# SP's loop over tile pairs written out in a four-layer graph network

## The reference

```python
# layer 0: softmax aggregation
m = relu(feat[src]) + 1e-7
a = exp(m - segment_max(m, dst)[dst]);  a = a / segment_sum(a, dst)[dst]
out = (feat + segment_sum(a * m, dst)) @ W + b
# layer 1: messages
edge_feat = mlp(edge_attr, W_edge, ...)          # relu, then a norm over all edges
message = mlp(concat([x[src], x[dst], edge_feat]), W_msg, ...)
out = segment_sum(message, dst) + mlp(x, W_node, ...)
# layers 2 and 3: two mean convolutions each, relu or elu between
agg = segment_sum(x[src], dst) / max(degree, 1)
out = agg @ Wl.T + b + x @ Wr.T
```

## Time and profile before

| | |
|---|---|
| median of 3 runs | 5197.18 us (5192.36 to 5201.1) |
| profiled execution, its own time | 5191.9 us |
| its span, first to last instruction | 5190.1 us |
| TensorE busy | 3237.4 us (62%) |
| VectorE busy | 2697.6 us (52%) |
| GpSimd busy | 2510.4 us (48%) |
| ScalarE busy | 1566.9 us (30%) |
| SP's hardware queue q1 | 239330 packets, 586.35 MB |
| mean traffic | 153 GB/s |

### The profile page before, as it was taken

How to read it: one execution, slowest core, us unless ns; L and a number is a source line. 1 busy time by engine, 2 the same in 40 slices (tenths; PEclk the granted TensorE clock), 3 DMA queues, 4 the chain that set the end, 5 groups by cost and what they waited for, 6 DMA issues and landing times.

```text
span 5190.1 us, 69196 instructions
## 1 busy us (share of the span) xinstructions
PE 3237.4 (62%) x18737; PEld 2376.6 (46%) x18737; DVE 2697.6 (52%) x5882; ACT 1566.9 (30%) x3677; POOL 2510.4 (48%) x2580
## 2 busy tenths in 40 slices
PE   1555555554656666556666664111159999999999
PEld 0333333333544444444444443100037777788777
DVE  4888888888545555555555556400001254433333
ACT  1777777775222222222222222100000011111000
POOL 7666666665466666666666666777720000000000
PEclk9999999999756766766676776555579999999999
DMA  5555555554134444444444443100037656676776
GB/s 182 191 196 194 194 195 195 194 196 153 48 93 110 113 115 114 113 110 115 114 110 112 117 112 91 60 0 0 13 113 283 224 209 246 246 254 247 260 277 227
DMA packets 387448, 796.21 MB, mean 153 GB/s; under 512 B 207412, under 2 KB 264600, under 8 KB 361128
## 3 DMA queue, kind: packets, MB, share of 16 engines
q1 hardware_dynamic: 239330, 586.35, 33.7%
q0 software_dynamic: 82320, 90.28, 8.2%
q10 hardware_dynamic: 65718, 118.62, 6.0%
HBM read 581.03 MB, written 213.92 MB: 153 GB/s over the span
## 4 chain that ended last, share of the span: by engine, by line
PE 28%; issue 19%; SPq 10%; another core or an unknown queue 7%; DVE 4%; ACT 2%; DMA 1%; ACTq 1%; DVEq 0%; POOL 0%
PE ps L1169 17%; PE ps L1099 6%; SPq L634 6%; ACT ps L1218 1%; PE ps L923 1%; SPq L609 1%; PE ps L930 1%; PE ps L929 1%; SPq L604 1%; SPq L625 1%; PE ps L1052 1%; DMA attr<-attr_parts 1%; SPq L615 1%; SPq L630 1%
## 5 line engine op out<-in xcount | busy, mean ns | idle before, releaser
L780 POOL DMA_INDIRECT area<-src_table,early x784 | 752.4, 960 | 480.1 <-remote 249.0
L780 POOL DMA_INDIRECT area<-relu_table,early x784 | 741.5, 946 | 413.2 <-issue 210.0
L941 PE MATMUL ps<-ident,area 96*128 96x96 f32 x2352 | 428.6, 348 | 429.6 <-issue 212.5
L1169 PE MATMUL ps<-second,area 128*128 128x288 bf16 x5194 | 650.7, 286 | 0.2 <-DVE second L1811 0.2
L941 PEld LDWEIGHTS ps<-ident,area 96*128 96x128 f32 x2352 | 347.6, 208 | 547.3 <-issue 402.8
L1169 PEld LDWEIGHTS ps<-second,area 128*128 128x128 f16 x5194 | 508.2, 98 | 127.7 <-DVE second L1811 0.5
L1632 DVE SCALAR_TENSOR_TENSOR second<-second,area,ps 128x512 bf16<-128x512 f32 x784 | 537.9, 741 | 0.0
L1664 DVE TENSOR_TENSOR_SCAN area<-flags,area,ps 96x512 f32<-96x512 int8 x196 | 250.0, 1276 | 534.3 <-ACT dump L1222 456.9
L929 PE MATMUL ps<-ident,area 128*96 128x128 f32 x1568 | 430.9, 370 | 112.4 <-issue 74.1
L929 PEld LDWEIGHTS ps<-ident,area 128*96 128x96 f32 x1568 | 335.8, 241 | 297.5 <-issue 246.7
L845 POOL DMA_INDIRECT adj<-out_ring x390 | 396.9, 1018 | 126.2 <-issue 126.2
(11 more groups left out here) (330 smaller groups left out, 4701.9 us busy)
## 6 DMA issues: line engine op xcount, KB each, us to landing
area<-adj SPq DMA_DIRECT2D x147, 1632.0 KB
area<-adj SPq DMA_DIRECT2D x55, 1568.0 KB
adj<-early SPq DMA_DIRECT2D x102, 816.0 KB
soft_sums<-out_ring ACTq DMA_DIRECT2D x196, 384.0 KB
second<-key_dram SPq DMA_DIRECT2D x98, 512.0 KB
area<-dst_table SPq DMA_DIRECT2D x784, 48.0 KB
sums<-out_ring ACTq DMA_DIRECT2D x196, 192.0 KB
second<-caps_dram SPq DMA_DIRECT2D x98, 192.0 KB
```

What stands on the lines that cost most here:

```text
L780: pool.indirect_dma_start(out=src_rows[:, s, c % CH, :], out_offset=None, in_=gather_table[p], in_offset=bass.IndirectOffsetOnAxis(ap=src_ ...
L941: last = nc.tensor.transpose(ps[:, b, c * F:(c + 1) * F], r[:, (s * CH + c) * P:(s * CH + c + 1) * P], ident[0:F, 0:F])
L1169: last = nc.tensor.matmul(bank(b, P, PARTS_F), slots[:, lane, s, :], y[:, s, :, :].rearrange("p c f -> p (c f)"), start=s == 0, stop=s == ...
```

## The change

In both passes the loop of SP is a Python loop, so that its 48 rounds are written out in SP's program, with constant addresses and constant counts in its waits. `load` itself is the same, and so are the programs of the other engines.

```diff
@@ -646,7 +646,7 @@
                     sp.wait_ge(later_stored, 16 * LATER_STORES)
                     sp.wait_ge(deg_made, 1)
                     sp.dma_start(node_cols, node_cols_in).then_inc(cells_in_landed, 16)
-                with sp.Fori(1, EI) as u:
+                for u in range(1, EI):
                     for h in range(RING // 2):
                         load(u, h)
```

## The result

| kernel, same chip | median | ratio to the kernel before |
|---|---|---|
| before | 5193.8 us (5189.1 to 5201.1) | |
| changed | 5199.9 us (5196.1 to 5213.4) | 1.0013 [1.0007, 1.0019] |

The forecast was 5096 us. The time went up by 6 us, inside the 0.2% that was called "no change". The profiled execution has a span of 5195.1 us, against 5190.1.

What follows compares the result with a forecast made beforehand. SP's instruction stream was taken to bound the message pass: 115 us saved there, 15 taken off as a guess, nothing for softmax pass or code. The 5197.2 us median less 100 gave 5097, stated as 5096; range 4940 to 5200.

Steps and rivals of the forecast that it cites:

- SP's instruction stream paces the message pass: Message pass: SP, always executing, sets the pace at 17.8 us a pair of tiles, no engine being full.
- s goes by GpSimd's 12 DMAs, thus by time: Message pass: SP's slow time s, 12.4 us a pair, follows GpSimd's DMAs and not SP's instruction count.
- the rest at 0.25 us shrinks with the instructions: Message pass: 16.6 instructions outside slow time cost 0.25 us each, 4.15 us, so a pair takes 16.6 us, 1.2 less.
- The term of 115 us: Message pass: 96 pairs of tiles, each 1.2 us shorter without SP's loop instructions, save 115 us.
- The 15 taken off: Message pass: a guessed 15 us less gain, for shorter GpSimd pauses and SP waiting for buffers, leaving 100 us.
- the bounds of 70 to 250: Message pass gain: 70 us if removed instructions lie in undisturbed time, at most 250 before GpSimd takes over.
- gives nothing: Softmax pass: no gain, as SP's removed instructions lie in its 790 us of waiting at L609.
- Code: SP's written-out stream, some 3,100 instructions: 24 or more extra q14 packets, fetched ahead, counted as no cost; bound 44 us.
- No gain: Rival, 13%: message pass slow time expands to take what was saved, or another wait ends where SP's did; 5187 to 5207.

Runs made afterwards that it cites:

- 15th: Changed kernel with two of GpSimd's indirect DMAs per pair of tiles instead of twelve in the message pass, on a chip with pauses: 4512.2 us, 0.868.
- first two experiments: Kernel before with only SP's softmax loop written out: 5179.5 us, 1.0035; with only SP's message loop written out: 5156.2 us, 0.9990.

## Why the prediction was wrong, point by point

- **"SP's instruction stream paces the message pass" is the step that failed.** It was read from SP having no waits and standing in the critical chain. Both are true, and after the change truer still. But SP can lose 18 more instructions (17.37 us) or gain 12 (17.89) and the pair hardly moves. The runs showed in its place that the pair follows GpSimd: with ten, eight and two of its twelve DMAs it takes 14.84, 12.57 and 10.56 us instead of 17.70. I had seen the evidence: GpSimd's pause of 2.80 us, and its 249 us at L780 in 109 waits (278 in 126 with the entry left out there). I took them for the room that a quicker SP would win, while 15.3 + 2.4 us was the pair itself.
- **"s goes by GpSimd's 12 DMAs, thus by time"**: half of it is confirmed. SP's slow stretches come with GpSimd's indirect DMAs (15th). But the other half of the sum, "the rest at 0.25 us shrinks with the instructions", is wrong: the pair's length is set elsewhere, so what is removed is filled again. The changed kernel's 29 instructions cost 0.61 us on average, the old 37.5 cost 0.475.
- **The term of 115 us** measured 10, and 7 on the chip of the first two experiments. The 15 taken off and the bounds of 70 to 250 had the same premise and fell with it.
- **The softmax pass, "gives nothing"**: it lost 15 us, on chips with pauses alone (1.0035 and 1.0043 there, 1.0000 on a chip without). It was costed as hidden by 790 us of waiting. SP's part is hidden; GpSimd's idle time in that pass rose from 193.2 to 208.7 us. Why is open.
- **Code**: q14 brought 66 packets instead of 43, and 34 instead of 13 in the message pass, 23 and 21 more where 24 and more were promised, and no gap of several microseconds appeared on SP (at most 1.4 between two of its instructions in the pass). Whether the 15 us above are its price is open. The preference for written-out code that the prediction took from the Trainium skill ("Runtime: NRT & Kernel Launch", instruction fetch) is not borne out here: 1.0013 with pauses, 0.9999 without.
- **The rivals**: "No gain" (13%), by which the slow time takes what was saved, is nearest to what happened, and 5199.9 lies in its 5187 to 5207. Its first wording, that the pauses would shrink, is true only in part: GpSimd's wait fell by 18 us and the pass by 10. The argument against it, that GpSimd itself waited 249 us, was an argument for it. Its chance was too low because the two readings of SP (cause or victim) were never weighed against each other.

What is shown: the slow instructions and late signals come with GpSimd's indirect DMAs; a pair grows and shrinks with their number, with 2.0 to 2.6 us of pauses beside them; SP's count has almost no bearing. What is only argued: that the pause is made by signals held back until GpSimd's run of DMAs has ended. Most rows above fit it, L904's signal doesn't, and no experiment moved a single signal by itself. What stays open: why some chips show this and others don't, and the 15 us of the softmax pass. None of the kernels with the whole computation beats the one before beyond what can be measured; the nearest, with only the message loop written out, has 0.9990 [0.9981, 0.9999].

## What to carry to other kernels

An engine that never waits and fills the critical chain isn't thereby the bound: ask whether its instructions have their undisturbed durations. If a MOVE of 29 ns takes 1400, its time is made by someone else, and removing instructions won't bring it back; adding or dropping some for one run tells at once. Look instead for an engine with a regular pause in each period. That its work and its pauses add up to the period says nothing yet, for they do so on every engine; take some of its work away, and if the pauses keep their size and the period shrinks, it sets the pace. Here each indirect DMA of GpSimd that was left out brought 1.1 to 1.4 us (17.70, 14.84 and 12.57 us for 12, 10 and 8).

## What the runs showed of the hardware that was not expected

The same kernel took 4501 us on two chips and 5163 to 5202 in the four other comparisons, with the instructions of VectorE, ScalarE and GpSimd nearly as long. The plainest place is behind the message pass, where GpSimd issues 390 scatters (L845) in a row, in which SP loads adjacency blocks (L676) and TensorE multiplies. The stretch of these scatters and SP's timeline in it, first on the chip of the result, then on one without pauses:

```profile
core 0: us, PE busy (x) PEld busy (x) DVE busy (x) ACT busy (x) POOL busy (x), PEclk, DMA share, GB/s
3293.00:3813.00 520.00, 78.74 (x251) 45.52 (x252) 40.98 (x80) 14.81 (x29) 396.63 (x389) 0.52 0.06 16
...
3305.33 420.65 SPq L676 DMA_DIRECT2D area<-adj  x5
```

```profile
2900.00:3405.00 505.00, 354.19 (x2491) 267.50 (x2491) 78.29 (x176) 13.89 (x29) 380.69 (x390) 0.84 0.46 156
...
2912.45 86.54 SPq L676 DMA_DIRECT2D area<-adj  x12
```

The stretch takes GpSimd 520 us instead of 505, 3% more. But SP started 5 loads in 421 us instead of 12 in 87, and TensorE ran 251 matmuls instead of 2491. It isn't a matter of full DMA engines, whose share in the slow stretch is 0.06. The 696 us between these two executions (spans of 5195.1 and 4499.6) lie so: 137 in the softmax pass (first to last L609), 17 up to the message pass, 259 in it, and 283 behind its last L609. The last part doesn't show in the stretch itself; it comes behind it, where the loads and matmuls have to be done that the other chip did beside the scatters (TensorE was busy there for 354 us, here for 79). An indirect DMA costs GpSimd 0.95 to 1.0 us on every chip; in four of the six comparisons it made the other engines' signals and SP's instructions slow as well. Whether it is the issuing or the transfer that does it, no run tells.
